# A transformer layer on one core: the last batch's output leaves in two column transfers, and the last attention addition is done by VectorE instead of GpSimd

## What is computed

```
h = take(W, x)                                   # 4 x 512 rows of 256
h = h + local_attention(layernorm(h)) @ Wo + bo  # 16 heads of 16, windows of 128
n = layernorm(h)
attn = full_attention(n)                         # 16 heads of 16, all 512 keys
moe = top-2 of 8 experts, weighted by the gate   # of n
out = h + (attn + moe)                           # (4, 512, 256) float32
```

## Time and profile before

| | us |
|---|---|
| median of 3 runs | 676.07 |
| lowest and highest of them | 670.94, 677.17 |
| the profiled execution's own time | 671.74 |
| its span, first to last instruction | 670.0 |
| TensorE busy in it | 550.9 |
| VectorE busy | 418.2 |
| ScalarE busy | 304.0 |
| GpSimd busy | 236.5 |

### The profile page before, as it was taken

The page is one execution under the profiler, slowest core; times in us unless marked ns, Lnnn a source line. Parts: engine busy times, 40 slices in busy tenths (PEclk is TensorE's granted clock), DMA queues, the critical chain, the costliest instruction groups (busy, mean ns, idle before and its releaser), DMA issues.

```text
span 670.0 us, 9773 instructions
## 1 busy us (share of the span) xinstructions
PE 550.9 (82%) x3352; PEld 280.3 (42%) x3352; DVE 418.2 (62%) x927; ACT 304.0 (45%) x570; POOL 236.5 (35%) x294
## 2 busy tenths in 40 slices
PE   4765998989999899998869899889948648999562
PEld 3443554755654344444424455443312224554110
DVE  7336756667687876676688557558836427757620
ACT  0312545536445655662433554346625414545452
POOL 3853235224223300215462324121164264430721
PEclk9968899899999999996967999999978788999957
DMA  6387515433532255233253486733263566851320
GB/s 166 110 174 154 115 49 159 80 64 96 112 81 83 91 144 126 77 99 95 76 170 109 152 210 200 188 96 94 72 165 95 141 188 174 275 166 49 87 71 32
DMA packets 48049, 81.81 MB, mean 122 GB/s; under 512 B 7672, under 2 KB 39040, under 8 KB 44928
## 3 DMA queue, kind: packets, MB, share of 16 engines
q1 hardware_dynamic: 40320, 58.11, 33.5%
q0 software_dynamic: 7680, 23.08, 11.7%
HBM read 52.59 MB, written 28.31 MB: 121 GB/s over the span
## 4 chain that ended last, share of the span: by engine, by line
PE 60%; DVE 20%; issue 10%; another core or an unknown queue 3%; ACT 2%; DMA 2%; POOL 1%; SPq 0%; POOLq 0%; DVEq 0%; ACTq 0%
PE OB L1441 11%; PE SC L1392 8%; PE R L1234 8%; DVE neg_max L933 6%; PE ST L1414 6%; PE R L1325 5%; PE R L1249 5%; PE SC L1397 3%; PE ST L1420 2%; DMA QS<-shiftT 2%; PE R L1310 2%; PE R L1282 2%; PE R L1340 2%; PE SC L1400 2%
## 5 line engine op out<-in xcount | busy, mean ns | idle before, releaser
L933 DVE TENSOR_REDUCE neg_max<-SC 128x1 f32<-128x512 f32 x256 | 169.5, 686 | 120.7 <-PE SC L1392 86.0
L800 ACT ACTIVATE prob<-ST 128x512 f32<-128x512 f32 x256 | 136.8, 600 | 106.4 <-PE ST L1414 84.3
L1392 PE MATMUL SC<-KS,QS 96*128 96x512 bf16 x256 | 99.4, 400 | 44.1 <-DVE neg_max L933 29.7
L1441 PE MATMUL OB<-prob,VS 128*32 128x512 f32 (+2 forms) x1024 | 113.4, 517 | 0.1
L803 ACT ACTIVATE prob<-ST 128x512 f32<-128x512 f32 (+1 forms) x128 | 68.6, 543 | 82.0 <-PE ST L1420 76.3
L1414 PE MATMUL ST<-QS,KS 98*128 98x512 bf16 x256 | 82.1, 396 | 13.8 <-issue 12.3
L672 POOL TENSOR_SCALAR_AFFINE_SELECT prob<-prob 128x512 f32<-128x512 f32 x64 | 41.0, 640 | 138.7 <-ACT prob L803 135.5
L1392 PEld LDWEIGHTS SC<-KS,QS 96*128 96x128 bf16 x256 | 25.2, 98 | 97.6 <-DVE neg_max L933 66.8
L941 DVE TENSOR_REDUCE neg_max<-SC 128x2 f32<-128x512 f32 x64 | 44.1, 688 | 24.8 <-PE SC L1400 24.4
L1397 PE MATMUL SC<-KS,QS 96*128 96x256 bf16 (+1 forms) x256 | 55.8, 271 | 2.9 <-DVE neg_max L938 1.7
L938 DVE TENSOR_REDUCE neg_max<-SC 128x1 f32<-128x128 f32 (+1 forms) x128 | 39.5, 350 | 28.0 <-PE SC L1400 26.6
(11 more groups left out here) (139 smaller groups left out, 816.1 us busy)
## 6 DMA issues: line engine op xcount, KB each, us to landing
scratch<-parts SPq DMA_DIRECT2D x96, 128.0 KB
QS<-scratch SPq DMA_DIRECT2D x16, 384.0 KB, 5.4
KS<-scratch SPq DMA_DIRECT2D x16, 384.0 KB, 4.7
xs<-x_sorted SPq DMA_DIRECT2D x24, 256.0 KB
y_sorted<-ys SPq DMA_DIRECT2D x24, 256.0 KB
QS<-scratch SPq DMA_DIRECT2D x16, 256.0 KB, 3.9
KS<-scratch SPq DMA_DIRECT2D x16, 256.0 KB, 4.9
x_sorted<-ys SPq DMA_DIRECT2D x24, 128.0 KB, 3.6
```

What stands on the lines that cost most here:

```text
L800: act.activation(prob[:, u % 2, e, :], src[:, :], ACT.Exp, scale=SCALE).then_inc(s_prob, 1)
L933: dve.tensor_reduce(own_max[:, i, head:head + 1], bank[:, :], AX.X, ALU.max, negate=True).then_inc(s_max, 1)
L1392: pe.matmul(bank[:, :], Q[0:SHIFT_ROW, head, i * P:(i + 1) * P], K[0:SHIFT_ROW, head, :], start=True, stop=True).then_inc(s_sc_ps, 1)
L1441: mm = pe.matmul(OB[VW * i:VW * (i + 1), columns], VS[s % 3][:, kt, v:v + VW], p_of, start=(kt == 0), stop=(kt == NT - 1), skip_group_chec ...
```

## The change

SP writes the last batch in two transfers: columns 0 to 191 of its four row tiles when three groups' attention is added, and columns 192 to 255 when the fourth is. The last group's addition moves from the end of GpSimd's stream to the end of VectorE's, behind `normalise` of the last group; it waits for its own last multiplication (`s_norm`) and for the 15 earlier attention additions of GpSimd (`s_yadd`). SP's new waits name `s_yadd` alone; the final wait counts one output transfer more.

```diff
@@ sync
+            def write_columns(first, end):
+
+                columns = slice(first * GH * HD, end * GH * HD)
+                sp.wait_ge(s_yadd, at(B - 1, G, end))
+                sp.dma_start(out_v[B - 1][:, :, columns], h[:, (B - 1) * NT:B * NT, columns]).then_inc(s_out, 16)
...
-            write_out(B - 1)
+            write_columns(0, G - 1)
+            write_columns(G - 1, G)
             for m in range(2):
                 sp.wait_ge(s_written[m], 32 * PARTS * len(STAGES))
             for k in range(Y_RING):
                 sp.wait_ge(s_stored[k], ring_count(2 * TILE_JOBS - Y_RING + k, Y_RING))
-            sp.wait_ge(s_out, 16 * B)
+            sp.wait_ge(s_out, 16 * (B + 1))
@@ gpsimd
                     if s == LAST and u >= UNITS - G + 1:
                         add_attention(B - 1, u - (UNITS - G + 1))
-            add_attention(B - 1, G - 1)
-
@@ vector
             normalise(G * len(STAGES) - 1)
+            dve.wait_ge(s_norm, G * len(STAGES))
+            dve.wait_ge(s_yadd, G * B - 1)
+            columns = slice((G - 1) * GH * HD, D)
+            rows = h[:, (B - 1) * NT:B * NT, columns]
+            dve.tensor_tensor(rows, rows, AF[:, :, columns], ALU.add).then_inc(s_yadd, 1)
```

## The result

The changed kernel takes 669.10 us (median of 20 runs, 666.36 to 674.47) where the kernel before takes 674.46 (20 runs, 669.59 to 677.85). The ratio is 0.9923 with a 95% interval of 0.9902 to 0.9944: 0.77% less, where 0.74% was forecast. The gain is real, and it is under the 1% that the prediction took as a bound. In us, 5.4 came where 5.0 were forecast; the forecast time of 671.1 lies 2.0 above the measured one mostly because it started from a median of three runs, 676.07, and twenty gave 674.46.

The account below looks back on a forecast made before the run. GpSimd's closing drain bounds the end: 655.51 + 9.24 = 664.75, plus 0.24 gives a span of 664.99 against 669.97, 5.0 us less; from the median of 676.07 that makes 671.1 us (0.74% less), range 665.5 to 675.5.

Parts of the forecast that it names:

- What bounds the end: At the block's closing, GpSimd's drain sets the span's end; the output transfer lies under it with 6.0 us to spare.
- The drain's 9.24 us behind the last instruction: At the block's closing, GpSimd's drain ends 9.24 us after its last instruction, so at 664.75 after the third addition.
- The alternative that I called equal within 0.1 us: GpSimd's closing drain: its length goes by its own dispatch, just as the instruction ahead begins; same sum within 0.1 us.
- the 173 ns: GpSimd's whole drain at the kernel's start, taken as a bound: the closing 9.24 us could shrink to about 0.1.
- SP from issue to DRAIN: Second output transfer, 128 KB: 1.6 us fixed plus 0.5 us of packets, from issue at 660.19 to SP's drain at 662.3.
- Packets: Second output transfer: 32 packets of 256 B on each engine, taken at 17 ns each, 0.5 us (0.3 to 1.5).
- Slack between SP and GpSimd: At the block's closing, GpSimd's drain still comes last, 2.4 us after SP's, so the shorter transfer itself gains nothing.
- The rule on packets under 512 B: Second output transfer, 256 B packets: speaks against the split; even at 93 ns each, the sum is unchanged within 0.1 us.
- The rule on a constant DRAIN of about 12 ns: Runtime's own DRAINs, all engines: by it rival B would hold; GpSimd's 9995 ns row disagrees; given only B's small chance.
- Rival A: GpSimd's closing drain waits for something neither kernel moves and ends where it did; nothing saved, 676.1 us; chance 0.14.
- B: GpSimd's closing drain shrinks with distance to earlier work; SP's path sets the end, 7.4 us less, 668.7 us; chance 0.05.
- C: Last stage: the early 384 KB transfer holds up an instruction fetch; 1.8 us longer, 677.9 us; chance 0.04.

Follow-up runs that it names:

- The small programs: Separate programs computing nothing of the reference, with GpSimd gathers and a last memset: closing drain 0.07 us behind it without gathers, 1.39 with 16.

## Why the prediction was right

- *What bounds the end.* Right. GpSimd's drain, not the output transfer, ended the span in every profile before and after, and moving GpSimd's last instruction ahead by 5.0 us moved the end by 5.0 us (11.02 to 6.03 behind TensorE's last matmul).
- *The drain's 9.24 us behind the last instruction.* Right as a constant of this kernel: 9.24 us in both profiles and in six further ones whose last instruction is an addition, 9.22 where it is a gather. The alternative that I called equal within 0.1 us, that it counts from its own dispatch, is wrong: the drain's row began at 658.5 and was 10.8 us long, since it was queued behind a running addition, so my 9.9 to 10.1 us for the row missed. The reading of the 173 ns was incomplete: it isn't that the end of a block is dear and its start cheap, but that at the start nothing had been issued. The small programs show it.
- *VectorE's addition*: 0.42 us (0.44 taken). *SP from issue to DRAIN*: 2.2 us (2.1). *Packets*: 18.9 ns (17), 0.6 us for 32 (0.5). *Slack between SP and GpSimd*: 2.3 us (2.4). All within 0.1 us.
- *The rule on packets under 512 B* (the Trainium skill, "DMA: Bandwidth & Descriptors", Specifications: full rate only from 512 B, below it a read-modify-write) could not have moved the time. Its first half the trace agrees with: 256 B packets cost 1.6 times as much by the byte as 1 KB ones. Whether a read-modify-write makes this the trace doesn't show; a small packet still took 18.9 ns, not the twice 46.5 that the prediction weighed.
- *The rule on a constant DRAIN of about 12 ns* (the Trainium skill, "VectorE: DVE Perf Modes", The DRAIN you can't avoid) is near SP's 7 ns, but GpSimd's takes 173 ns and 176 ns even with nothing issued, and 9.24 us behind its last instruction in this kernel.
- *Rival A* (the drain ends where it did) is out by the profile after; *B* (it shrinks) too, as put: what shrinks it is fewer transfers since the drain before, not distance. *C* (the early transfer holds up a fetch): ScalarE's unnamed stops are there with and without the change, and nothing stood still while the 384 KB moved (VectorE's 5.75 us ahead of the last reciprocal is what it was).
- *What I hadn't seen.* I wrote that the third addition is long over, and that nothing moves it, as if that held wherever the kernel runs. It holds where ScalarE stops in the last stage, as in the profile I had (9.2 us). Without such a stop GpSimd's additions wait for the experts' outputs, and the same change is worth 0.7 us, 0.1%. I read that stop as a danger (rival C) and not as a condition of my own sum. That the result was taken where ScalarE stops, so that 0.74% met 0.77% and not 0.1%, is luck: nothing in my working spoke for it but the one profile. Where ScalarE doesn't stop, GpSimd's drain sets the end all the same, but the 5.0 us are 0.7.

## What to carry to other kernels

When a kernel ends, look at each engine's closing drain before the last transfer: a GpSimd that has issued indirect transfers needs time behind its last instruction (9.2 us here after 112 or more, 1.4 after 16), and that may cover the output entirely. Then the cheapest gain is to let GpSimd finish early: give its last arithmetic to an idle engine, as with all four additions on VectorE (ratio 0.988). A drain of its own where GpSimd waits anyway shortens the last one (shown); that it shortens a kernel is not shown here. Ask of every slack that the sum uses which stall makes it, and whether that stall is there in every execution.

## What was unexpected of the hardware

- GpSimd's drain goes by the indirect transfers issued since the drain before: 0.07, 1.39 and 9.2 us behind the last instruction for 0, 16 and 112, that is 82 ns each, and a drain in the middle takes its share off the last. With 128 it was 9.24, so the line doesn't go on; where it bends is open.
- One program takes 671 to 674 us on some chips and 625 us on others. Of ScalarE's time, 41 to 45 us are waits for an unnamed releaser on the former and none on the latter, and VectorE and GpSimd have some too; their cause is open.
